# Moving copies, buffers and coefficients around in an attention and entropy-model kernel

## The reference

```python
# layer 0: group norm over 32 groups, then attention over the 4096 pixels
q = prelu(conv1x1(xn, w1, b1), a1)      # 24 channels
k = prelu(conv1x1(xn, w2, b2), a2)      # 24 channels
v = prelu(conv1x1(xn, wa, ba), aa)      # 192 channels
score = softmax(einsum('bnc,bcm->bnm', q, k), axis=2)
x = x + einsum('bnm,bmc->bnc', score, v)
# layer 1: group norm, then an entropy model, per channel, at xn - 0.5 and xn + 0.5
for i in range(4):                      # widths 1, 3, 3, 3, 1
    logits = softplus(m[i]) @ logits + b[i]
    if i < 3: logits = logits + tanh(f[i]) * tanh(logits)
likelihood = max(|sigmoid(sign*upper) - sigmoid(sign*lower)|, 1e-6)   # sign = -sign(lower + upper)
x = x + likelihood
```

## Time and profile before

| | |
|---|---|
| median of 3 runs | 5378.04 us (5373.47 to 5390.06) |
| the profiled execution | 5397.69 us, span 5395.8 us |
| PE busy | 4701.7 us, 87% |
| DVE busy | 4136.5 us, 77% |
| ACT busy | 3725.4 us, 69% |
| POOL busy | 788.6 us, 15% |
| DMA | 305.21 MB, 57 GB/s on average |

### The profile page before, as it was taken

How to read it: one execution, slowest core, us unless ns; L and a number is a source line. 1 busy time by engine, 2 the same in 40 slices (tenths; PEclk the granted TensorE clock), 3 DMA queues, 4 the chain that set the end, 5 groups by cost and what they waited for, 6 DMA issues and landing times.

```text
span 5395.8 us, 105296 instructions
## 1 busy us (share of the span) xinstructions
PE 4701.7 (87%) x38408; PEld 3094.8 (57%) x38408; DVE 4136.5 (77%) x5378; ACT 3725.4 (69%) x4117; POOL 788.6 (15%) x934
## 2 busy tenths in 40 slices
PE   2799879998799987999879998899888998789966
PEld 1588516783177732777338862487525885267821
DVE  2788678886798767887678867788677885789855
ACT  1466686666866678666876668766687666876677
POOL 6000230003200032000320013100131002310012
PEclk7899999999999999999999999999999999999988
DMA  2100331004400044001430014300232003320033
GB/s 47 30 19 19 87 114 46 16 16 105 128 14 19 24 110 114 18 13 36 113 100 16 19 48 117 83 13 19 69 111 67 19 19 79 115 51 14 19 100 94
DMA packets 107342, 305.21 MB, mean 57 GB/s; under 512 B 14401, under 2 KB 14785, under 8 KB 105090
## 3 DMA queue, kind: packets, MB, share of 16 engines
q1 hardware_dynamic: 106818, 298.01, 20.5%
HBM read 230.65 MB, written 50.33 MB: 52 GB/s over the span
## 4 chain that ended last, share of the span: by engine, by line
PE 56%; ACT 11%; issue 11%; DMA 10%; DVE 9%; POOL 2%; SPq 1%; DVEq 0%; ACTq 0%; POOLq 0%
PE ps L1236 11%; PE ps L1234 11%; PE ps L1238 10%; DMA arena<-x2d 9%; PE ps L1024 7%; PE ps L1189 7%; ACT th L584 6%; PE ps L1113 4%; ACT arena L578 2%; DVE th L866 2%; PE ps L1097 2%; DVE mxp L924 2%; DVE arena L919 1%; PE ps L1017 1%; PE ps L1043 1%
## 5 line engine op out<-in xcount | busy, mean ns | idle before, releaser
L1234 PE MATMUL ps<-v_sb,arena 128*128 128x193 f16 x8192 | 2028.2, 248 | 11.3 <-ACT lu L592 5.8
L1236 PE MATMUL ps<-v_sb,arena 128*128 128x192 f16 x8192 | 2036.5, 249 | 0.0
L1238 PE MATMUL ps<-v_sb,arena 128*128 128x193 f16 x8192 | 2019.6, 247 | 0.0
L546 ACT ACTIVATE arena<-ps 128x1024 f16<-128x1024 f32 x1024 | 1051.1, 1026 | 1001.8 <-PE ps L1024 1001.5
L919 DVE TENSOR_TENSOR arena<-arena 128x1024 f16<-128x1024 f32 x1024 | 1247.5, 1218 | 252.2 <-ACT arena L549 251.0
L924 DVE TENSOR_REDUCE mxp<-ps 128x1 f32<-128x512 f32 x1792 | 1189.8, 688 | 133.1 <-PE ps L1189 121.1
L866 DVE SCALAR_TENSOR_TENSOR th<-th,gates,ps 128x1024 f32<-128x1024 f32 x768 | 950.5, 1276 | 364.0 <-ACT th L584 361.9
L549 ACT ACTIVATE arena<-ps 128x1024 f32<-128x1024 f32 x1024 | 1046.9, 1022 | 0.0
L1236 PEld LDWEIGHTS ps<-v_sb,arena 128*128 128x128 f16 x8192 | 799.8, 98 | 265.8 <-issue 8.2
L1234 PEld LDWEIGHTS ps<-v_sb,arena 128*128 128x128 f16 x8192 | 796.6, 97 | 140.7 <-DVE arena L919 10.4
L584 ACT ACTIVATE th<-ps,biases 128x1024 f32<-128x1024 f32 x768 | 818.5, 1118 | 38.2 <-PE ps L1083 24.5
(11 more groups left out here) (122 smaller groups left out, 3442.0 us busy)
## 6 DMA issues: line engine op xcount, KB each, us to landing
arena<-x2d SPq DMA_DIRECT2D x384, 256.0 KB
arena<-x2d SPq DMA_DIRECT2D x384, 128.0 KB, 3.8
xp<-x_dram SPq DMA_DIRECT2D x18, 1536.0 KB, 14.2
xr<-x_dram SPq DMA_DIRECT2D x64, 384.0 KB, 3.5
x2d<-xr SPq DMA_DIRECT2D x64, 384.0 KB, 3.1
res<-x2d SPq DMA_DIRECT2D x96, 256.0 KB
out_dram<-res SPq DMA_DIRECT2D x96, 256.0 KB
kst<-kq SPq DMA_DIRECT2D x32, 256.0 KB, 4.8
```

The lines of the kernel that those rows point to most:

```text
L546: act.activation(e_hi[:, q % 4, :].rearrange("p (k n) -> p k n", k=2), sc, ACT.Exp)
L1234: pe.matmul(acc, eh, v_sb[:, m, 0:C + 1], start=(m == 0 and t % 2 == 0), stop=False, skip_group_check=True)
L1236: pe.matmul(acc[:, 0:C], eh, v_sb[:, m, VW:VW + C], start=False, stop=False, skip_group_check=True)
L1238: ins = pe.matmul(acc, el, v_sb[:, m, 0:C + 1], start=False, stop=(m == MT - 1), skip_group_check=True)
```

## The change

- **Coefficients:** POOL computes them after its part of the start's phase_a. PE waits for them only in an image's phase_a.
- **Value banks:** V_LEAD = 6 of them come ahead of slot 0 (before 2), the others in slots 0 to 9.
- **x4:** three buffers; x4(0) and x4(2) are issued at the start of the image, x4(v + 3) after the tanhs of v.
- **Side rows** of half-units 0 and 1 are loaded ahead of the tanhs, whose four first instructions become eight that leave out the side rows' partitions.
- **Stack copies:** one DMA for each of v = 2 to 11. The maxima move to slots 26 to 41.
- **Memory:** kq shares its memory with xr. POOL's first casts wait for the x2 stores, and SP waits for the stack copies before it loads xr. th2 has six slots.
- **Order:** on PE, qk_bank(0) comes behind turn_out (L1017) of the last block. ACT has the relus of banks 5 to 8 between its first tanhs, one behind each.

```diff
-T0R, HR1, HR2, XR = 3, 2, 5, 4
+X4R, T0R, HR1, HR2, XR = 3, 3, 2, 6, 4
+SPLIT = 2
+V_LEAD = 6
-FIRST_AT = 18
+FIRST_AT = 26
-        kq = sb("kq", [P, HW], F16)
-        xr = sb("xr", [HALF, 2, 2, N])
+        shared = sb("shared", [P, 4 * N])
+        xr = shared[0:HALF, :].rearrange("p (s h n) -> p s h n", s=2, h=2)
+        kq = shared[:, :].bitcast(F16)
-        arena = sb("arena", [P, 8 * HC])
-        x4 = arena[:, 0:2 * HC].rearrange("p (s n) -> p s n", s=2)
-        t0 = arena[:, 2 * HC:8 * HC].rearrange("p (s d n) -> p s d n", s=T0R, d=2)
+        arena = sb("arena", [P, (X4R + 2 * T0R) * HC])
+        x4 = arena[:, 0:X4R * HC].rearrange("p (s n) -> p s n", s=X4R)
+        t0 = arena[:, X4R * HC:(X4R + 2 * T0R) * HC].rearrange("p (s d n) -> p s d n", s=T0R, d=2)
...
             def load_side(l, row, v):
-                sp.wait_ge(t0_ready, l * SLOTS + 2 * v + 2)
+                if v >= SPLIT:
+                    sp.wait_ge(t0_ready, l * SLOTS + 2 * v + 2)
...
-                def stack(i):
-                    sp.wait_ge(qk_done, pj(QK, 4 * i + 4))
+                def stack(i, part):
+                    if part == 0:
+                        sp.wait_ge(qk_done, pj(QK, 4 * i + 4))
...
-                if l is not None:
+                if l is None:
+                    for i in range(2):
+                        for part in range(STACK_DMAS):
+                            stack(i, part)
+                else:
                     load_x4(l, row, 0)
+                    load_x4(l, row, 2)
+                    sp.wait_ge(summed, l * BLOCKS * PAIRS + BLOCKS * PAIRS)
+                    load_side(l, row, 0)
                     store_x2(l, row, BLOCKS - 1)
                     for s in range(2):
                         sp.wait_ge(x2_stored[s], l * 64 + 64)
                     load_x4(l, row, 1)
-                elif proj:
-                    stack(0)
-                    stack(1)
-                if l is not None:
+                    load_side(l, row, 1)
                     for v in range(HALVES):
-                        load_side(l, row, v)
-                        if v + 2 < HALVES:
-                            load_x4(l, row, v + 2)
+                        if v >= SPLIT:
+                            load_side(l, row, v)
+                        elif v + X4R < HALVES:
+                            sp.wait_ge(t0_ready, l * SLOTS + 2 * v + 2)
+                        if v + X4R < HALVES:
+                            load_x4(l, row, v + X4R)
                         if v >= 8 and v % 2 == 0:
                             store(l, row, v // 2 - 4)
                         if v % 2 == 1:
                             load_res(l, row, v // 2)
-                        if proj and v in (2, 4):
-                            stack(v // 2 - 1)
+                        if proj and 2 <= v < 2 + 2 * STACK_DMAS:
+                            stack((v - 2) // STACK_DMAS, (v - 2) % STACK_DMAS)
...
+                for i in range(2):
+                    sp.wait_ge(stacks_in[i], b * STACK_DMAS * 16 + STACK_DMAS * 16)
...
-                        pool.wait_ge(stacks_in[n // 4], l * STACK_DMAS * 16 + STACK_DMAS * 16)
+                        pool.wait_ge(x2_stored[n // 4], l * 64 + 64)
...
-                    for v in range(2):
+                    for v in range(V_LEAD):
                         values(v)
...
             phase_a(None, True)
+            coefficients()
             with pool.Fori(0, B - 1) as b:
...
-                    act.activation(t0[:, v % T0R, d, :], x4[:, v % 2, :], ACT.Tanh, bias=biases[:, d, 0, u:u + 1],
-                                   scale=scl[:, u:u + 1]).then_inc(t0_ready, 1)
+                    for lo, hi in ((0, 48), (64, 112)) if v < SPLIT else ((0, P),):
+                        ins = act.activation(t0[lo:hi, v % T0R, d, :], x4[lo:hi, v % X4R, :], ACT.Tanh,
+                                             bias=biases[lo:hi, d, 0, u:u + 1], scale=scl[lo:hi, u:u + 1])
+                    ins.then_inc(t0_ready, 1)
...
-                    first_tanh(0)
-                    first_tanh(1)
-                    for i in range(2, LEAD):
+                    for i in range(LEAD):
+                        first_tanh(i)
                         if proj:
-                            negative(3 + i)
-                        first_tanh(i)
+                            negative(5 + i)
...
-                    if proj:
-                        qk_bank(0)
                     pe.wait_ge(out_norm, l * BLOCKS + BLOCKS + START)
                     pe.wait_ge(x2_ready, l * 2 * BLOCKS + 2 * BLOCKS - 2 + START)
                     for h in range(2):
                         turn_out(1, h, 5 - h)
                     if proj:
+                        qk_bank(0)
                         qk_bank(1)
...
-                    value_bank(0)
-                    value_bank(1)
-                pe.wait_ge(set_gp, 3)
+                    for v in range(V_LEAD):
+                        value_bank(v)
+                if l is not None:
+                    pe.wait_ge(set_gp, 3)
```

More of the change, by code:

```diff
@@ L234, in program @@
         x2_stored = [sem(f"x2_stored{s}") for s in range(2)]
-        x4_in = [sem(f"x4_in{s}") for s in range(2)]
+        x4_in = [sem(f"x4_in{s}") for s in range(X4R)]
         t0_ready = sem("t0_ready")
@@ L285, in load_x4 @@
                     col = (v % 2 * 2 + a) * HC
-                    sp.dma_start(x4[64 * a:64 * a + 64, v % 2, :],
+                    sp.dma_start(x4[64 * a:64 * a + 64, v % X4R, :],
                                  x2d[bass.ds(row + v // 2 * UC, UC), col:col + HC].unsqueeze(0)
-                                 .to_broadcast([4, UC, HC])).then_inc(x4_in[v % 2], 16)
+                                 .to_broadcast([4, UC, HC])).then_inc(x4_in[v % X4R], 16)
             def load_side(l, row, v):
-                sp.wait_ge(t0_ready, l * SLOTS + 2 * v + 2)
+                if v >= SPLIT:
+                    sp.wait_ge(t0_ready, l * SLOTS + 2 * v + 2)
                 for a in range(2):
@@ L312, in phase_a @@
                 pj = counter(l)
-                def stack(i):
-                    sp.wait_ge(qk_done, pj(QK, 4 * i + 4))
+                def stack(i, part):
+                    if part == 0:
+                        sp.wait_ge(qk_done, pj(QK, 4 * i + 4))
                     w = HW // 2
[L317 to L321, removed]
+                    dst, to, first, rows = ((kst, 0, 0, 2), (qst, 2, 2, 2), (kst, 2, 0, 2), (qst, 0, 3, 1),
+                                            (qst, 1, 2, 1))[part]
+                    sp.dma_start(dst[to * SUB:(to + rows) * SUB, i * w:(i + 1) * w],
+                                 kq[first * SUB:(first + rows) * SUB, i * w:(i + 1) * w]).then_inc(stacks_in[i], 16)
                 def rows_in(j):
@@ L410, in _ @@
             pool.wait_ge(set_gp, 2)
[L411 to L434, removed]
@@ L437, in _ @@
[L437 to L442, removed]
-                for i in range(HID):
[L444 to L450, removed]
@@ L495, in phase_a @@
                         queries(n)
-                    for v in range(2):
+                    for v in range(V_LEAD):
                         values(v)
                 for s in range(SLOTS + 6):
-                    if proj and s + 2 < VB:
-                        values(s + 2)
+                    if proj and s + V_LEAD < VB:
+                        values(s + V_LEAD)
                     u = (s - 5) // 4
@@ L604, in phase_a @@
                 if proj:
-                    for n in range(3, 5 if l is not None else QK + 2):
+                    for n in range(3, 5 if l is not None else QK + V_LEAD):
                         negative(n)
@@ L608, in phase_a @@
                     act.wait_ge(gn2_step, l * GN2_STEPS + 16)
-                    first_tanh(0)
-                    first_tanh(1)
-                    for i in range(2, LEAD):
+                    for i in range(LEAD):
+                        first_tanh(i)
                         if proj:
-                            negative(3 + i)
-                        first_tanh(i)
+                            negative(5 + i)
                     if proj:
-                        for n in range(3 + LEAD, QK + 2):
+                        for n in range(5 + LEAD, QK + V_LEAD):
                             negative(n)
@@ L640, in phase_a @@
                                 sigmoid(l, u)
-                    if proj and s + 2 < VB:
-                        negative(QK + s + 2)
+                    if proj and s + V_LEAD < VB:
+                        negative(QK + s + V_LEAD)
                 if proj:
@@ L869, in phase_a @@
                 if l is None:
-                    for n in range(QK + 2):
+                    for n in range(QK + V_LEAD):
                         query(n)
@@ L892, in phase_a @@
                     if proj:
-                        for n in range(4, QK + 2):
+                        for n in range(4, QK + V_LEAD):
```

(8 more changed lines are left out.)

40 lines of the change are left out of this document (38 added, 2 removed).

## The result

Four runs of the changed kernel have a median of 5414.58 us (5410.09 to 5423.41) against 5377.11 us before: ratio 1.0067, 95% interval 1.0046 to 1.0089. The forecast was 5286. The loss is small, but clear of the spread of the runs. The profiled execution has a span of 5421.4 us, 25.6 more than before. Lines of the file have moved: the first tanh is L596, the h1 and h2 tanhs L603, first-layer matmuls L1100, side rows L300, x4 L290, res loads L310, the last x2 store L284 and SP's wait for it L344.

What follows compares the result with a forecast made beforehand. It took ACT, held up by x4 copies that fill four of sixteen DMA engines, to bound the entropy model. Gains of 54.5 (start) + 7 x 5 (images) + 3 (last image) = 92 us from 5378 gave 5286; 80% range 5225 to 5345.

Steps and rivals of the forecast that it cites:

- (1): Start of the kernel: coefficients after the first projections remove the stop of ACT's relus, 54.5 us gained once.
- (2): Prelude of an image, first tanh to first h1 tanh: x4(1) arrives late, first h1 tanh 13 us later than before.
- (3): Slots of an image: longer lead for x4 copies, end at 1471 against 1475.9, 5 us gained per image with projections.
- The DMA term: Slots of image 1: copies of x4(5) to x4(23) take 177 us, to 1449; 22.1 us more give the end, 1471.
- the sign of being wrong that the prediction had named: Slots: the forecast is wrong if a half-unit late in the image takes over 9 us.
- rival C: Prelude and slots: late third tanh holds up value banks, slots keep their length, 12 us lost per image: 5420; chance 5%.
- the sum of 8.9 us per half-unit: Slots, load on four DMA engines: 6.9 for x4, 1.0 for side rows, 1.0 for res load and store; measured period 8.93.
- The reading of the four engines: x4 copies in the entropy model: they run on 4 of 16 DMA engines, which are full; a third buffer adds none.
- A: Rival on prelude and slots: four engines already full, late start just made good, only the start won: 5324; chance 23%.
- B: Rival on x4 copies: they aren't the limit, the store isn't held up, 15 us gained per image: 5204; chance 17%.
- (4): Last image, without value banks: x4(1) again 8 us late, 3 us gained (-5 to +10).
- (5): Other moves (spread stack copies, later maxima, kq in xr's place, sixth th2 slot): put at nothing.

Runs made afterwards that it cites:

- e1: Kernel before with only the coefficients moved behind POOL's start part: 5328.57 us against 5385.98, ratio 0.9891.
- e5: Changed kernel with each res load a half-unit later, behind that half-unit's store: 5402.15 us, ratio 1.0034 to the kernel before.
- e2: Changed kernel with each x4 copy of 64 partitions issued as four of 16 partitions: 5255.23 us, ratio 0.9757 to the kernel before.
- e8: Kernel before with the coefficients later and each x4 copy issued as four of 16 partitions, two x4 buffers: 5220.2 us, ratio 0.9694.
- e10: Changed kernel with each x4 copy cut by columns into four, each still a broadcast to 64 partitions: 5494.53 us, ratio 1.0188 to the kernel before.
- e13: Changed kernel with x4(2) behind x4(1), two value banks ahead and whole first tanhs: 5317.33 us, ratio 0.9888 to the kernel before.
- e11: Changed kernel with x4 copies as four of 16 partitions, whole first tanhs, two value banks ahead: 5218.28 us, ratio 0.9700 to the kernel before.

## Why the prediction was wrong

- **(1) The start: right.** 54.5 us forecast, 54.6 measured, and alone some 59 us by e1's ratio (interval 50 to 68).
- **(2) The prelude: right in mechanism, too small.** First h1 tanh 29.3 us behind the first tanh in image 1, 25.8 forecast. The store behind two x4 pairs, the third tanh's wait for x4(1), the tanhs that get no cheaper with fewer partitions and the slow clock after it are all there. The wait for the store was forecast to end 13.5 us after its issue and took 13.8. Most of what was under-priced is x4(1) itself: the third tanh ran 11.3 us after its issue (9.0 forecast), and so 13.0 us behind the first (10.7 forecast); from there to the slots it took 16.3 us instead of 15.1. The forecast made the prelude 14 us longer (13, with 1 us won ahead of it); in the mean it is 17.2 longer. In the last image it is 11.1 instead of 8.
- **(3) The slots: this is the step that failed.** Forecast 206 us (1264.6 to 1471), 17.9 less than before; measured 218 in image 1, 5.6 less in the mean. Of the 118 us between the 92 forecast as gained and the 26 lost, 86 lie here. The DMA term nearly held: I gave the copies from the sixth tanh to x4(23) 177 us; they went from 1234.13, and at 1413.5 all engines but one fell idle, 179 us later. What did not hold is what I tied to its end. I let the tanh that needs the last x4 copy start as that copy lands, 22.1 us ahead of the end of the slots, as before. But with a third buffer each copy is issued a half-unit ahead of its old place. The tanh for x4(23) ran at 1423.01, without a wait and 9.5 us after the engines fell idle, and the end came 23.4 us behind it: these 9.5 us are most of the 12. Counted with a half-unit of 9 us more, the prediction's own terms give 215 us (an estimate).
- **What took the place of the wait for x4.** ACT's pace without x4 waits was put at 8.34 us per half-unit; in image 1 a half-unit takes 218.2 / 24 = 9.1 us. By the timelines, from one half-unit's first h1 tanh to the next, the first nine took 9.25 us each instead of 10.40, but the last fourteen 9.26 instead of 8.95: the sign of being wrong that the prediction had named. Only x4 got a longer lead. The side rows are still issued behind a half-unit's second tanh and needed three slots later, and they pass through the same full rings. By SP's order, two x4 pairs can now be ahead of them where it was one; in the changed kernel they are what is late (83.4 to 168.5 us). I had written that side rows and x4 queue on the same full engines only in rival C, and priced it at nothing in the forecast. I also overlooked SP's wait for a store ahead of each res load (78 to 315 us); e5 shows that it is worth little. ACT, SP and PE near the end of image 1's slots:

```profile
1400.78 0.79 SPq L300 DMA_DIRECT2D arena<-x2d  x2
...
1410.81 1.09 PE L1100 MATMUL ps<-arena,w1s 64*64 64x512 f32 x8 [2.17 <-DMA arena<-x2d]
...
1418.46 0.66 SPq L310 DMA_DIRECT2D res<-x2d  x1
1419.30 0.79 SPq L300 DMA_DIRECT2D arena<-x2d  x2
...
1423.01 1.24 ACT L596 ACTIVATE arena<-arena,biases,scl 128x1024 f32<-128x1024 f32 x1
```

Counted back from the last half-unit, the side rows of half-unit 20 are issued at 1400.78, and PE, idle for 2.17 us, starts its first layer at 1410.81, 10.0 us later. Those of half-unit 22 go out at 1419.30, behind a res load that waited for a store.

One term of the sum of 8.9 us per half-unit was also too small. Loads and stores of res were priced at the 264 GB/s of the x2 store. The last store of results is alone in the rings (length, granted clock, DMA share, GB/s):

```profile
5419.00:5420.00 1.00, 0.50 0.48 150
```

It holds the share at 0.48, eight of sixteen engines, and moves 150 GB/s, so that 256 KB take some 1.7 us rather than 1.0 (an estimate from this row, if the loads go like the stores). With that the sum is 9.6 us, over the 8.93 measured: the terms don't simply add, and that 8.9 met 8.93 was in part luck. That the four engines are what is full is shown by e2 and e8, not by this sum.

- **The rivals.** C had the right sign and nearly the time (5420): the late third tanh, six banks on a PE at the lower clock, the slots keep most of their length; its loss of 12 us per image is the measured 11.6. It put the first h1 tanh 18 us later and left the slots at 218 us (224 less 2 and 4), against 17.2 and 218 measured. I gave it 5% since waits for x4 stood in the trace and I took their removal for a gain. The reading of the four engines, which stood in the text as speaking against the change, was the right one: e2 against the changed kernel, and e8 against e1, differ in the form of the x4 copies alone, and e10's side rows say that it is not their number. By the Trainium skill, "DMA: Bandwidth & Descriptors", section "Why a DMA increments its semaphore by 16 and not by 1", a copy of 16 rows to 16 partitions may use all sixteen engines and the broadcast only four. The trace agrees that it is more than four: x4 copies alone hold the share at 0.49 in e2, against 0.25.
- A (5324) had the full engines right, but counted the late start as made good; only 5.6 of its 17.2 us were. e13, in which the first h1 tanh comes 13.3 us behind the first tanh, ends at A's time.
- B (5204) needed copies that are no limit. That kernel exists, but as e8 and e11, at 0.970 of the time, and not by another buffer.
- **(4)** forecast 3 us gained in the last image (its own terms give 209.6 - 200 - 8 = 1.6); 7.5 were lost, 11.1 in the prelude against 3.6 won in the slots. **(5)** held: the maxima are in time, and e13 finds nothing in the other moves. Between the images 1.1 us each were won; e1, in which qk_bank(0) keeps its place, has 0.8 of them, so little is left for that move, which wasn't tried alone.

## What to carry to other kernels

When a transfer is late, ask first whether it is issued late or served slowly. A buffer can help only with the first; against a full ring it moves the wait to whatever is next on the same ring with no lead of its own. A mean DMA share of 0.4 can hide four engines that are full: look for a floor in the share (here 0.25), and at the outermost dimension of both sides of the copy. Before putting work ahead of a loop that fills a wait, see what stands behind it in each queue.

## What the runs showed that I had not expected

- Cutting one broadcast copy into four plain ones of 16 partitions makes the kernel 2.0% faster (0.9891 to 0.9694), although SP issues four times as many.
- An activation on 48 partitions takes as long as on 128: 1237 and 1248 ns.
- From 1413.5 to 1418.5 the DMA share is 0.07, one engine of sixteen, and SP's wait for a result store, issued at 1403.25, ends right then (1418.46). In the trace that one engine works off packets of 4096 bytes, the size of the x4 copies' and side rows', until 1416.7, and only then packets of 2048 bytes, the size of the store's. Why this engine was so far behind the others is open.
